# First attention's queries as three products of two-part tokens and weights

## The reference

```python
def _L0_xattn_ref(queries, keys, values, mask, Wq, bq, Wk, bk, Wv, bv, Wo, bo):
    q = split_heads(queries @ Wq + bq)
    k = split_heads(keys @ Wk + bk)
    v = split_heads(values @ Wv + bv)
    scores = jnp.einsum('bhqd,bhkd->bhqk', q, k) / jnp.sqrt(jnp.float32(HD))
    scores = jnp.where(mask, jnp.float32(-1000000000000000.0), scores)
    ...
x = x + jnp.tanh(g_xattn[0]) * _L0_xattn_ref(_layernorm(x, axis=-1), ctx_1024, ctx_1024, mask_Bx1xSxS2_bk1, ...)
```

## Time and profile before

| | us |
|---|---|
| device time, three runs | 853.56, 854.37, 856.18 |
| median | 854.37 |
| the profiled execution's own time | 851.03 |
| its span, first to last instruction | 848.9 |

### The profile page before, as it was taken

One profiled execution on the slowest core, in us unless ns is written; L12 is line 12 of the kernel. 1 busy time (PEld: TensorE's weight loads), 2 busy tenths in 40 slices (PEclk: granted clock), 3 DMA queues, 4 the chain that ended last, 5 costly groups with the idle time before them and its releaser, 6 DMA issues.

```text
span 848.9 us, 22217 instructions
## 1 busy us (share of the span) xinstructions
PE 770.1 (91%) x7992; PEld 602.9 (71%) x7992; DVE 580.6 (68%) x1773; ACT 470.7 (55%) x1014; POOL 218.2 (26%) x212
## 2 busy tenths in 40 slices
PE   5879999999999888779998679998999998889997
PEld 2547777777777665469996457777777776569996
DVE  4877778777787677744545778887888777574433
ACT  2455665656556467335663346665666666555553
POOL 2562322133232305700005444224312112010000
PEclk9999999999999999989999869999999999899999
DMA  8898878678776904623325778887978888000001
GB/s 197 178 231 208 179 162 162 147 164 177 163 172 139 217 8 126 186 84 101 119 91 131 154 159 167 203 173 150 201 171 182 188 188 184 12 1 1 20 20 39
DMA packets 153765, 117.87 MB, mean 139 GB/s; under 512 B 81574, under 2 KB 145170, under 8 KB 153650
## 3 DMA queue, kind: packets, MB, share of 16 engines
q1 hardware_dynamic: 146410, 107.93, 56.1%
q0 software_dynamic: 4096, 6.57, 3.1%
q10 hardware_dynamic: 3152, 1.96, 1.0%
HBM read 76.17 MB, written 38.30 MB: 135 GB/s over the span
## 4 chain that ended last, share of the span: by engine, by line
PE 68%; DVE 12%; DMA 5%; issue 4%; ACT 4%; SPq 4%; ACTq 1%; POOL 1%; DVEq 0%; POOLq 0%
PE ps L1981 21%; PE ps L2125 9%; PE ps L2099 8%; PE ps L2158 6%; PE ps L2148 6%; PE ps L2182 3%; PE ps L2144 3%; DVE mx L1589 2%; DVE ps L1585 2%; DMA scr_q<-qp 2%; ACT prob L1020 2%; PE ps L2052 2%; DMA QS<-scr_q 1%; PE ps L2168 1%; PE ps L2040 1%
## 5 line engine op out<-in xcount | busy, mean ns | idle before, releaser
L1020 ACT ACTIVATE prob<-ps 128x400 f32<-128x400 f32 (+1 forms) x384 | 182.3, 499 | 87.6 <-PE ps L2148 81.1
L2125 PE MATMUL ps<-KS,QS 96*100 96x361 bf16 x512 | 164.9, 338 | 16.1 <-DMA QS<-qp 4.7
L1585 DVE CUSTOM_DVE_ANT_0 ps<-ps,biasq 100x361 f32<-100x361 f32 x256 | 135.3, 542 | 50.7 <-PE ps L2125 46.8
L1589 DVE TENSOR_REDUCE mx<-ps 100x1 f32<-100x361 f32 x256 | 126.9, 527 | 42.2 <-PE ps L2125 41.2
L2148 PEld LDWEIGHTS ps<-QS,KS 98*128 98x128 bf16 x1536 | 108.7, 100 | 50.1 <-ACT prob L1020 8.9
L2148 PE MATMUL ps<-QS,KS 98*128 98x100 bf16 x1536 | 133.2, 210 | 7.5 <-ACT prob L1020 4.6
L2099 PE MATMUL ps<-cT,wk 128*128 128x361 f32 x256 | 96.2, 486 | 7.5 <-PEq L2394 6.8
L2125 PEld LDWEIGHTS ps<-KS,QS 96*100 96x100 bf16 x512 | 63.8, 126 | 51.3 <-DVE mx L1589 15.4
L730 POOL TENSOR_TENSOR kp<-kr,kp 128x722 bf16<-128x722 f32 x32 | 48.7, 1521 | 184.8 <-ACT kp L991 184.6
L2158 PE MATMUL ps<-prob,V 128*17 128x100 f32 (+1 forms) x3072 | 82.0, 256 | 0.1
L2158 PEld LDWEIGHTS ps<-prob,V 128*17 128x17 f32 (+1 forms) x3072 | 66.5, 99 | 12.6 <-issue 9.4
(11 more groups left out here) (225 smaller groups left out, 1610.8 us busy)
## 6 DMA issues: line engine op xcount, KB each, us to landing
scr_k<-kp SPq DMA_DIRECT2D x93, 180.5 KB, 4.2
KS<-scr_k SPq DMA_DIRECT2D x62, 270.8 KB, 4.0
cT<-in_ctxT SPq DMA_DIRECT2D x32, 361.0 KB, 4.3
KS<-scr_k SPq DMA_DIRECT2D x62, 180.5 KB, 4.2
QS<-scr_q SPq DMA_DIRECT2D x60, 150.0 KB, 3.9
KS<-scr_k SPq DMA_DIRECT2D x62, 90.2 KB, 4.4
scr_q<-qp SPq DMA_DIRECT2D x42, 100.0 KB, 4.6
xg<-scr_x SPq DMA_DIRECT2D x32, 128.0 KB
```

Of the source, the lines that this page charges most:

```text
L1020: nc.scalar.activation(prob[0:KROWS[t], t, hg, :], ps[0:KROWS[t], c % 2, 0:HQ * S], ACT.Exp).then_inc(a["exp"], 1)
L1585: nc.vector.tensor_tensor_reduce(ps[0:S, banks[h % len(banks)], 0:S2], ps[0:S, banks[h % len(banks)], 0:S2], biasq[p][:, :], 1.0, -3.0e38, ...
L1589: nc.vector.reduce_max(mx[:, h:h + 1], ps[0:S, banks[h % len(banks)], 0:S2], axis=AX.X).then_inc(a["max"], 1)
L2125: mm(ps[0:S, banks[h % len(banks)], 0:S2], QS[p][0:SROWS, h, :], KS[p][0:SROWS, h * S2:(h + 1) * S2], start=True, stop=True).then_inc(a["s ...
```

## The change

For the first attention alone, tokens and Wq are each kept in two float32r parts and the plain float32 product is replaced by `split_mm`.

- ScalarE writes the scaled Wq as float32r to a new tile `wqh` in place of over itself, and writes the turned tokens of Q0 as float32r to `xTr`, a second view of the place of `xT`.
- VectorE gets five new instructions: `wq_low` (128 x 512: Wq times the scale, less `wqh`) and `first_tokens_low(g)` for the four groups (128 x 800: the turned tokens in PSUM, less `xTr`). They stand at written-out places in its order, and count `s1["xl"]` up, five times in all.
- TensorE waits for `s1["xl"]` ahead of each group's queries (group 2 for all four groups' rests), and ahead of turning groups 1 to 3, since the rest reads the banks that the next group's turning overwrites. Each matmul of `project_q` becomes three products.
- The new tiles `xql`, `wqh`, `wql` lie in the place of `prob`. In `up1` the count waited for is raised by five.

```diff
 overlay("token_place", ...)   # xT as float32, xTr as float32r, one place
...
             def norm(p, g):
...
-                nc.scalar.activation(xT[:, :, g * GT:(g + 1) * GT], ps[:, bank:bank + KT, 0:GT], ACT.Copy).then_inc(sn["xT"], 1)
+                nc.scalar.activation((xTr if p == Q0 else xT)[:, :, g * GT:(g + 1) * GT], ps[:, bank:bank + KT, 0:GT], ACT.Copy).then_inc(sn["xT"], 1)
...
-                nc.scalar.activation(w_attn[l]["q"][:, :, :], w_attn[l]["q"][:, :, :], ACT.Copy, scale=SCALE).then_inc(s_wq[l], 1)
+                nc.scalar.activation((w_attn[l]["q"] if l else wqh)[:, :, :], w_attn[l]["q"][:, :, :], ACT.Copy, scale=SCALE).then_inc(s_wq[l], 1)
...
+            def wq_low():
+                dve.wait_ge(s_wq[0], 2)
+                nc.vector.scalar_tensor_tensor(wql[:, :, :], w_attn[0]["q"][:, :, :], SCALE, wqh[:, :, :].bitcast(F32),
+                                               ALU.mult, ALU.subtract).then_inc(s1["xl"], 1)
+
+            def first_tokens_low(g):
+                dve.wait_ge(sn["xT"], START + g + 1)
+                nc.vector.tensor_tensor(xql[:, :, g * GT:(g + 1) * GT], ps[:, NBANKS[Q0][g]:NBANKS[Q0][g] + KT, 0:GT],
+                                        xTr[:, :, g * GT:(g + 1) * GT].bitcast(F32), ALU.subtract).then_inc(s1["xl"], 1)
...
                     stats_x(0)
                     norm(Q0, 0)
+                    wq_low()
                     k_rest(l, 0, 0)
                     stats_x(1)
+                    first_tokens_low(0)
                     k_rest(l, 0, 1)
                     q_rest(l, 0)
                     norm(Q0, 1)
                     wv_low(0)
                     ctx_low(0, 0, 0)
+                    first_tokens_low(1)
                     q_rest(l, 1)
...
                 maxima(l, 0, 0, 0, 4, SBANKS0)
                 if l == 0:
+                    first_tokens_low(2)
                     norm(Q0, GE)
...
-                maxima(l, 0, 0, 4, (12, 9)[l], SBANKS0)
+                if l == 0:
+                    maxima(l, 0, 0, 4, 8, SBANKS0)
+                    first_tokens_low(GE)
+                    maxima(l, 0, 0, 8, 12, SBANKS0)
+                else:
+                    maxima(l, 0, 0, 4, 9, SBANKS0)
...
+                if p == Q0 and g > 0:
+                    pe.wait_ge(s1["xl"], START + 1 + g)
...
-            def project_q(l, g, m):
+            def project_q(g, m):
                 q = sq[g % 2]
                 if m == 0:
-                    pe.wait_ge(sn["xT"], START + (NG if g == 2 else g + 1))
+                    pe.wait_ge(s1["xl"], START + 1 + (NG if g == 2 else g + 1))
...
                 for k in range(KT):
-                    x = mm(ps[:, QBANK[g] + m, 0:GT], w_attn[l]["q"][:, k, m * P:(m + 1) * P],
-                           xT[:, k, g * GT:(g + 1) * GT], start=k == 0, stop=k == KT - 1)
+                    cols, t = slice(m * P, (m + 1) * P), slice(g * GT, (g + 1) * GT)
+                    x = split_mm(ps[:, QBANK[g] + m, 0:GT], (wqh[:, k, cols], wql[:, k, cols]), (xTr[:, k, t], xql[:, k, t]),
+                                 k == 0, k == KT - 1)
...
-                    pe.wait_ge(s1["xl"], START + g + 1)
+                    pe.wait_ge(s1["xl"], START + NQLOW + g + 1)
```

More of the change, by code:

```diff
@@ L102, in build @@
         xn = sb("xn", [S, GB, D])
-        xT = sb("xT", [P, KT, B * S])
         scr_q = dram("scr_q", [KT, NST, P, B * S], BF16)
@@ L182, in asb @@
             return ctx.enter_context(nc.sbuf_tensor(name, shape, dt))
+        overlay("token_place", [("xT", [P, KT, B * S], F32)], [("xTr", [P, KT, B * S], F32R)])
+        xT, xTr = T["xT"], T["xTr"]
         overlay("parts_place",
@@ L202, in build @@
                 [("prob", [P, NKT, NHG, HQ * S], F32)],
+                [("xql", [P, KT, B * S], F32R), ("wqh", [P, KT, D], F32R), ("wql", [P, KT, D], F32R)],
                 [(f"{n}{p}", shape, dt) for n, shape, dt in (
@@ L225, in build @@
         kp, kr, lgT, yT, prob, xn4, yg = (T[n] for n in ("kp", "kr", "lgT", "yT", "prob", "xn4", "yg"))
+        xql, wqh, wql = (T[n] for n in ("xql", "wqh", "wql"))
         xh, xl = ([T[f"{n}{p}"] for p in range(2)] for n in ("xh", "xl"))
@@ L366, in build @@
         NKEPT = 3
+        NQLOW = NG + 1
         s_held = sem("held_waits")
@@ L2042, in project_pair @@
                 x.then_inc(q["ready"], 1)
-            def project_q(l, g, m):
+            def project_q(g, m):
                 q = sq[g % 2]
                 if m == 0:
-                    pe.wait_ge(sn["xT"], START + (NG if g == 2 else g + 1))
+                    pe.wait_ge(s1["xl"], START + 1 + (NG if g == 2 else g + 1))
                     if g == 3:
-                        pe.wait_ge(sq[0]["rest1"], START + KT * JQ * (l + 1))
+                        pe.wait_ge(sq[0]["rest1"], START + KT * JQ)
                 for k in range(KT):
-                    x = mm(ps[:, QBANK[g] + m, 0:GT], w_attn[l]["q"][:, k, m * P:(m + 1) * P],
-                           xT[:, k, g * GT:(g + 1) * GT], start=k == 0, stop=k == KT - 1)
+                    cols, t = slice(m * P, (m + 1) * P), slice(g * GT, (g + 1) * GT)
+                    x = split_mm(ps[:, QBANK[g] + m, 0:GT], (wqh[:, k, cols], wql[:, k, cols]), (xTr[:, k, t], xql[:, k, t]),
+                                 k == 0, k == KT - 1)
                 x.then_inc(q["ready"], 1)
@@ L2293, in queries @@
                     for m in range(KT):
-                        project_q(l, g, m)
+                        project_q(g, m)
                 if l == 0:
@@ L2337, in attn @@
                     if l == 0 and h in Q2_AT:
-                        project_q(l, 2, Q2_AT.index(h))
+                        project_q(2, Q2_AT.index(h))
                 values(1, 1, range(2))
```

## The result

| | before | changed |
|---|---|---|
| median, us | 854.8 (853.56 to 856.18, 4 runs) | 862.13 (860.38 to 868.85, 4 runs) |
| ratio, 95% interval | | 1.0095 [1.0061, 1.0130] |
| the same two kernels again (e11), median, us | 848.01 (27 runs) | 857.21 (10 runs) |
| ratio, 95% interval | | 1.0094 [1.0053, 1.0136] |
| profiled execution: time, span, us | 851.03, 848.9 | 860.38, 858.3 |

The change makes the kernel 0.95% slower, some 8 us (0.0095 x 854.8); the interval goes from 5 to 11 us, and the medians lie 7.3 us apart here and 9.2 us in e11. The forecast was 7.1 us and 861.5 us. The profiled execution of e7 was one of the slow kind (856.0 us, where the median of its twelve is 847.8), so neither its length nor its start-up is compared.

A forecast was written before the change was run, and what follows sets the result against it. Before 54 us no engine is full, so the chain of waits between engines was taken to bound the kernel there. Terms 5.6 + 2.2 - 0.7 = 7.1 us on the median of 854.37 gave 861.5 us, range 856.7 to 864.8.

The forecast's parts named there:

- Queries 0: First query group: starts 2.8 us later behind VectorE's rests, runs at the slow clock, what follows stands at +2.3 us.
- Queries 1: Second query group: starts 5.0 us later, nine of twelve products slow, ends at +5.6 us (between +4.2 and +6.0).
- Groups 2 and 3: Among the heads, paced by VectorE: waits and rests of tokens add 2.2 us net, from 0 to 3.3.
- Queries 3: Last query group, on the chain alone at the fast clock: 2.2 in place of 2.92 us, -0.7 us.
- Sum: Whole kernel: 5.6 + 2.2 - 0.7 = 7.1 us slower, giving 861.5 us.
- Edits at nothing: New ScalarE targets, the place of `prob`, waits ahead of turning groups 1 to 3, SyncE and GpSimd issue: no cost.
- The clock rival: Queries 1 run at the fast clock, 1.4 us less than forecast: 860.1 us; chance 0.17.
- The rival of the faster kernel: At queries 0 and 1, VectorE makes rests in idle time, shorter products gain: 851.7 us; chance 0.08.

The follow-up runs named there:

- e11: The changed kernel run again, unaltered, beside the kernel before; ratio to the kernel before 1.0094 [1.0053, 1.0136].
- e7: The kernel before, plus extra identity matmuls in TensorE's idle time ahead of turning groups 0 and 1 and queries 0 and 1; ratio 0.9993 [0.9963, 1.0023].
- e3: The changed kernel with all rests made, but high parts multiplied three times and queries 0, 1 and 3 not waiting for rests; ratio to before 1.0046.
- e10: As e3, but VectorE makes the rests of Wq and group 0 behind both rests of the first keys; ratio to the kernel before 1.0025.
- e4: The changed kernel plus extra identity matmuls in TensorE's idle time ahead of queries 0, turning group 1 and queries 1; ratio to before 1.0092.
- e6: As e5, plus extra identity matmuls in TensorE's idle time and the rest of group 2 moved behind norm(Q0, 3); ratio to before 1.0017.
- e5: The changed kernel reordered: group 0's rest ahead of group 1's statistics, group 1's tokens and rest ahead of context 0's; ratio to before 1.0065.
- e1: The changed kernel without rests and waits for them, the three products multiplying the high parts; ratio to before 1.0029 [0.9993, 1.0065].
- e8: The changed kernel with rests and three products only for groups 2 and 3 and Wq, queries 0 and 1 one plain matmul; ratio to before 1.0042.

## Why the prediction was right

- *Queries 0.* The order on VectorE was as worked out: rest of Wq 0.69, rest of tokens 0.96 us (taken 0.7 and 1.0), TensorE 2.80 us later relative to the turning (forecast 2.8). The slow clock was taken rightly, by the spacing of the products and by e11's PEclk of 0.50. The products were mis-sized: 12 x 0.33 = 4.0 us was set against a measured 4.50 that holds the way to the last copy; like for like it was 4.38 against 4.53 us. So ScalarE's second copy stood at +2.65 (22.29 - 12.63 against 19.30 - 12.29), not at +2.3.
- *Queries 1.* Start +5.2 (forecast +5.0). At ScalarE's last copy +6.6, where +5.6 was forecast and +6.0 the upper bound: all twelve products were slow, not nine, and the tail of 0.4 us was missing here too. That nothing up to the maxima gives it back held: the first maximum stood at +6.6 as well.
- *Groups 2 and 3.* +3.1 (from the first maximum to `q_rest(2)`: 13.02 us before, 16.17 changed), forecast +2.2 with 3.3 above (the terms as written add up to 2.3). The wait of 0.54 us, the rests (0.99 and 0.98) and the shorter `norm` (1.62 in place of 2.14) were as worked out. What was missed is a third slow stretch: PEclk was 0.50 from 47 to 53 us, after TensorE had worked 2.3 of the 4 us from 44 to 48 and none of the next, queries 2 took 0.33 us for each product, and VectorE waited 1.92 us for head 10 where 0.5 was forecast (1.9 us or more in all nine profiles with these rests and waits, at most 0.36 in those without). The text had queries 2 as "covered by VectorE", and said that three of the four groups are on the chain. That was misread: queries 2 were on it before the change (39.58 and 41.46 us), and what waited for them was priced too low.
- *Queries 3.* -0.6 (forecast -0.7), at the fast clock as said.
- *Sum.* 6.6 + 3.1 - 0.6 = 9.1 us in the profile against 7.1 forecast, some 8 us in the times. The mechanism held ahead of queries 0 and 1; among the heads the rests and waits were as written and queries 2 were misplaced. Each of the two large errors made a term too small, by the clock and by the tail of a group. That the median came out within 0.6 us of 861.5 is luck in part: the start-up was 2.0 us longer than forecast, and e11 puts the same two kernels 9.2 us apart.
- *Edits at nothing.* The working let only VectorE's work and TensorE's waits count, which was too simple. e3 and e10 show a path that the text did not name: VectorE's order also holds ScalarE, and through it GpSimd. In the changed kernel it lies beside the longer wait of TensorE (`norm(Q0, 1)` follows `q_rest(0)` at 23.47 us and waits for nobody, GpSimd's deviation being done at 21.98), so it costs nothing on top; with the wait gone it costs 3.1 us (e3 against e10).
- *The clock rival* (queries 1 fast) needed help: it came about only with fills (e4, e6). *The rival of the faster kernel* had its deciding point right: in e5 the rests end earlier and a third of the start-up's loss goes, in e6 with a better clock more than half. But even e1, with no rests at all, was not faster: of that rival's 2.7 us nothing was left in its start-up, and queries 1 ran partly at the slow clock (3.75 us where some 2.2 were reckoned).

Open: how the 9.1 us of the start-up split between clock and order in the measured times. The fills change both what TensorE does and its clock, and the times tell 0.35%, not 1 us. Open too is why the clock falls in one profile and holds in another where TensorE's work looks alike.

## What to carry to other kernels

Where an engine is not full, price a new instruction by what stands behind it in its own queue and then in the queues of those who wait for that, not by its length: two instructions of 1.65 us on VectorE cost 3.1 us more of the start-up in one place than in another (e3, e10). Look as well at what an engine meets when it comes earlier or later: more than half of these 3.1 us came from a normalization that met GpSimd's work. A part that one engine needs next goes ahead of statistics and copies that have time. And a saving in products can be lost to a slower clock, as in e1: look at PEclk in the burst, and at the spacing of equal products, which showed the slow level where PEclk did not.

## What the runs showed of the hardware

- *Shorter products, a slower clock.* In e1 the granted clock fell to 0.50 between queries 0 and 1, where with the longer plain products it had held, and queries 1 took 3.75 us in place of 2.97. This is one profile each. That the shorter products are the cause is not shown, and e8 speaks against it as the whole cause: its queries 0 and 1 are plain matmuls with no wait for rests, and queries 1 ran at 0.50 all the same.
- *PEclk can read 1.00 over slow products.* In queries 0 of the changed kernel, twelve products 0.33 us apart in both profiles, PEclk 1.00 in one and 0.50 in the other.
- *VectorE beside GpSimd.* The four instructions of one `norm` (100 x 256 each) took 1.37 us alone, 3.09 us beside a GpSimd instruction of 1.70 us (e3) and 2.93 us beside one of 1.73 us (e7).
- *The expert stage is not of constant length*, though no kernel here changes it. VectorE's product of gates and values, first to last start, before and in e5:

```profile
L1844 DVE TENSOR_TENSOR hx<-ps,sg x48: 339/357/359, 331.3 to 454.9; 128x192 f32<-128x192 f32 x32, 100x192 f32<-100x192 f32 x16
```

```profile
L1868 DVE TENSOR_TENSOR hx<-ps,sg x48: 338/358/359, 337.7 to 453.4; 128x192 f32<-128x192 f32 x32, 100x192 f32<-100x192 f32 x16
```

123.6 and 115.7 us, and 115.7 to 124.3 us over all profiles. This is as large as the effect of the change; that is why the start-up was compared and not the spans. Its cause was not looked for.
